# A DLRM tower on one core: gathers tied to TensorE's steps, padded id lines, another order of steps

## The reference

```python
e = jnp.stack([tbl_0[ids[:, 0]], ..., tbl_25[ids[:, 25]]], axis=1)
all_emb = jnp.concatenate([bottom_output[:, None, :], embeddings], axis=1)
gram = jnp.einsum('bfd,bgd->bfg', all_emb, all_emb)
z = gram[:, _TRIU_I, _TRIU_J]
...
h = jnp.concatenate([z, r_bottom_output], axis=1)
h = jnp.maximum(h @ W_top1 + b_top1, 0.0)      # 479 -> 512
h = jnp.maximum(h @ W_top2 + b_top2, 0.0)      # 512 -> 256
y = h @ W_top3                                 # 256 -> 1
```

## Time and profile before

| | us |
|---|---|
| median of 3 runs | 500.98 |
| the runs | 501.84, 500.98, 497.73 |
| the profiled execution: from its first to its last instruction | 370.7 |
| median minus that span | 130.3 |
| PE, PEld, DVE, ACT, POOL busy | 343.2, 282.3, 236.3, 230.8, 257.2 |
| granted clock of TensorE, mean | 0.963 |

### The profile page before, as it was taken

One profiled execution on the slowest core, in us unless ns is written; L12 is line 12 of the kernel. 1 busy time (PEld: TensorE's weight loads), 2 busy tenths in 40 slices (PEclk: granted clock), 3 DMA queues, 4 the chain that ended last, 5 costly groups with the idle time before them and its releaser, 6 DMA issues.

```text
span 370.7 us, 8525 instructions
## 1 busy us (share of the span) xinstructions
PE 343.2 (93%) x3422; PEld 282.3 (76%) x3422; DVE 236.3 (64%) x312; ACT 230.8 (62%) x298; POOL 257.2 (69%) x261
## 2 busy tenths in 40 slices
PE   6899999999699999999999999997977996899996
PEld 5688888887587778788788877776866785677886
DVE  2999999999497769798789945313340332522452
ACT  2699989888497896499997833447321473223222
POOL 5777878777777777777877877777777777770010
PEclk9699999999699999999999999999896999899999
DMA  6977687665957789988767629534593425323200
GB/s 174 249 217 211 194 248 222 190 198 163 319 112 251 205 242 341 287 235 252 230 156 245 191 77 347 176 96 114 152 366 99 115 74 146 97 52 85 66 20 2
DMA packets 48391, 66.86 MB, mean 180 GB/s; under 512 B 15861, under 2 KB 34847, under 8 KB 47840
## 3 DMA queue, kind: packets, MB, share of 16 engines
q1 hardware_dynamic: 40024, 49.32, 43.9%
q0 software_dynamic: 8064, 16.31, 16.7%
q10 hardware_dynamic: 264, 0.69, 0.6%
HBM read 52.36 MB, written 13.93 MB: 179 GB/s over the span
## 4 chain that ended last, share of the span: by engine, by line
PE 69%; POOL 10%; DMA 6%; ACT 5%; issue 5%; DVE 3%; SPq 1%; ACTq 0%; DVEq 0%
PE acc L624 21%; PE acc L625 21%; POOL rows L591 10%; PE gram L655 9%; PE turned L637 6%; PE acc L660 4%; PE acc L661 4%; PE acc L662 4%; DMA rows<-in_tbl,index 2%; DMA wanted<-in_onehot_ids 2%; DVE onehot L899 2%; ACT features L741 1%; ACT staged L823 1%; ACT h L769 1%; DMA square<-products 1%
## 5 line engine op out<-in xcount | busy, mean ns | idle before, releaser
L591 POOL DMA_INDIRECT rows<-in_tbl,index x248 | 253.9, 1024 | 77.7 <-issue 74.4
L899 DVE TENSOR_SCALAR onehot<-wanted,row_number 125x1029 fp32r<-125x1029 int32 (+3 forms) x137 | 151.0, 1150 | 19.6 <-PE acc L625 13.3
L624 PE MATMUL acc<-onehot,table_hi 125*128 125x512 f32 x336 | 136.6, 407 | 3.1 <-DVE table_lo L893 3.1
L625 PE MATMUL acc<-onehot,table_lo 125*128 125x512 f32 x288 | 115.7, 402 | 0.0
L624 PEld LDWEIGHTS acc<-onehot,table_hi 125*128 125x128 f32 x336 | 64.7, 193 | 17.8 <-DVE table_lo L893 3.3
L655 PEld LDWEIGHTS gram<-features 128*54 128x54 f32 x2048 | 60.6, 136 | 17.6 <-issue 14.6
L655 PE MATMUL gram<-features 128*54 128x52 f32 x2048 | 67.5, 222 | 6.0 <-DVE features L925 3.0
L625 PEld LDWEIGHTS acc<-onehot,table_lo 125*128 125x128 f32 x288 | 55.7, 194 | 12.4
L769 ACT ACTIVATE h<-wanted,row_number 125x1029 f32<-125x1029 int32 x42 | 48.8, 1163 | 23.4 <-PE acc L625 20.3
L637 PE MATMUL turned<-identity,rows 128*128 128x128 f32 x248 | 41.8, 294 | 9.9 <-DMA rows<-in_tbl,index 8.1
L772 ACT ACTIVATE onehot<-h,row_number 125x1029 fp32r<-125x1029 f32 x42 | 48.6, 1157 | 1.4
(11 more groups left out here) (49 smaller groups left out, 285.4 us busy)
## 6 DMA issues: line engine op xcount, KB each, us to landing
wanted<-in_onehot_ids SPq DMA_DIRECT2D x20, 514.5 KB, 6.0
parked<-staged SPq DMA_DIRECT2D x32, 256.0 KB, 4.3
table_raw<-in_tbl SPq DMA_DIRECT2D x17, 448.0 KB
looked<-parked SPq DMA_DIRECT2D x2, 2816.0 KB, 12.4
square<-products SPq DMA_DIRECT2D x62, 84.5 KB
rows<-in_tbl,index POOLq DMA_INDIRECT x248
looked<-parked SPq DMA_DIRECT2D x1, 2560.0 KB, 11.0
pairs<-in_tbl SPq DMA_DIRECT2D x3, 448.0 KB
```

The lines of the kernel that those rows point to most:

```text
L591: pool.indirect_dma_start(out=rows[:, n % ROWS_RING, i, :], out_offset=None, in_=gathered[f], in_offset=bass.IndirectOffsetOnAxis(ap=index ...
L624: pe.matmul(to, table_hi[0:ROW_PARTS, v % HIGH_RING, c, :], of, start=(c == 0), stop=False)
L625: last = pe.matmul(to, raw_table(v, low=True)[0:ROW_PARTS, c, :], of, start=False, stop=(c == CHUNKS - 1))
L899: return dve.tensor_scalar(column[:, rows], ids_of(v, slice(0, ROW_PARTS))[:, rows], row_number[0:ROW_PARTS, c:c + 1], None, ALU.is_equal)
```

## The change

1. `order` also lists, for each gather, the step of TensorE that by plan ends at least 3 us (6 us from tile 13 on) before the gather would begin, and GpSimd waits for that step ahead of the gather (`keep_pace`). A wait that repeats the one before it is left out; 192 are left. By the planned lengths gathers 0 to 7 have none, gather 13 waits for column 7 of lookup 0, gather 40 (the first of turn (2, 2)) for column 7 of lookup 4, gather 229 for gram (13, 0), gathers 242 to 244 for gram (14, 0) and 245 to 247 for gram (14, 1).
2. The ids lie in memory in padded lines, as they lie in the core: a partition's copy is one run of 4144 bytes instead of seven of 588 (for lookup 0 one of 2368 and one of 1776).
3. VectorE's round: low half 0 of the next table comes ahead of its columns 0 and 1.
4. The slot-0 fills of the first block come ahead of lookup 9 on VectorE, those of later tiles one tile after another. ScalarE copies the first nine slots of tile 0 (`place_ahead`) ahead of a column of the next lookup instead of after it.
5. The end: turns (15, 2) and (15, 3) come ahead of layer2 of part 2, which is done in two halves, the second after gram (15, 3); an output comes behind the first quarter of the next part's layer1; the pairs of part 3 are loaded after layer1 of part 2; `h2` lies in the place of `table_hi`, so that pairs may be split before the output is done.

```diff
@@ products_and_others
-    steps = [("lookup", v, 0) for v in range(FIRST_LATER)]
+    steps = [("lookup", v, 0) for v in range(FIRST_LATER - 1)]
+    steps += [("bottom", q, 0) for q in range(BLOCK_TILES)] + [("lookup", FIRST_LATER - 1, 0)]
...
-            before += [[] for _ in range(LAYERS_AT[b] - LOOKUPS_AMONG[b])] + layers(b - 1) + [[("output", b - 1, 0)]]
+            before += [[] for _ in range(LAYERS_AT[b] - LOOKUPS_AMONG[b])] + layers(b - 1)
+            before += [[("output", b - 1, 0)]] if b - 1 != APART else []
...
+            if BLOCK_TILES <= chunk[1] + 1 < TILES and chunk[2] == 0:
+                steps.append(("bottom", chunk[1] + 1, 0))
...
+    steps += [("layer2", APART, 1)]
     for part in range(BLOCKS - 1, len(PARTS)):
-        steps += [step for place in layers(part) for step in place] + [("output", part, 0)]
-    return steps
+        steps += begun(part) + [("output", part - 1, 0)] + rest(part)
+    return steps + [("output", len(PARTS) - 1, 0)]
@@ order
+        begins.extend((step[1], gathered - GATHER_LANDS + i * GATHER_LENGTH) for i in range(groups_of(step[1])[step[2]]))
...
+        while step == ("layer2", APART, 0) and turns:
+            turn()
...
+    for t, begin in begins:
+        paces.append(max(((end, step) for end, step in ended if end <= begin - PACE_LEAD[t >= LATE_TILES]),
+                         default=(0, None))[1])
@@ loads of pairs
-PAIRS_AFTER["gram", TILES - 2, TILE_CHUNKS - 1] = (len(PARTS) - 2, 0, BLOCK_TILES - 1)
+PAIRS_AFTER["layer1", APART, M1 - 1] = (len(PARTS) - 2, 0, EARLY_TILES)
+PAIRS_AFTER["gram", TILES - 2, TILE_CHUNKS - 1] = (len(PARTS) - 1, EARLY_TILES, BLOCK_TILES - 1)
@@ ids, SyncE
-                    sp.dma_start(ids_of(v, slice(0, P)), onehot_ids[i:i + 1, first:first + WIDTH].to_broadcast([P, WIDTH])
-                                 ).then_inc(wanted_landed[v % WANTED_RING], 16)
+                    sp.dma_start(to, of.to_broadcast([P, ID_LINE])).then_inc(wanted_landed[v % WANTED_RING], 16)
@@ GpSimd
+            def keep_pace(n):
+                if PACES[n] is None or n and PACES[n] == PACES[n - 1]:
+                    return
+                kind, x, y = PACES[n]
+                if kind == "lookup" and y < CHUNKS - 1:
+                    pool.wait_ge(onehot_used, x * (CHUNKS - 1) + y + 1)
+                elif kind == "lookup":
+                    pool.wait_ge(accumulated, visited(x))
+                else:
+                    pool.wait_ge(grammed, x * TILE_CHUNKS + y + 1)
...
                         f = GROUP * g + i
+                        keep_pace(gathers_before(t) + f)
                         pool.indirect_dma_start(
@@ VectorE
                     if x + 1 < len(VISITS):
+                        table_low_part(x + 1, 0)
                         build(x + 1, (0, 1))
-                        table_low_part(x + 1, 0)
                         build(x + 1, (3,))
...
-                    dve.wait_ge(accumulated, FILL["output", last_on_tiles_of(part), 0] + 1)
+                    dve.wait_ge(accumulated, FILL["layer1", last_on_tiles_of(part), M1 - 1] + 1)
@@ ScalarE
+                    if x == FIRST_LATER - 1:
+                        place_ahead(x)
                     if more:
                         act_chunk(x + 1, ACT_COLUMNS[0])
```

More of the change, by code:

```diff
@@ L49 @@
 WIDE_RING = 6
+ID_LINE = ID_ROWS * ID_PITCH
 FIRST_ROWS = 4
@@ L136, with outputs_of @@
 LAYERS_AT = (None, 10, 10, 8)
+APART = BLOCKS - 2
+def outputs_of(part, i):
+    return (i,) if part == APART else tuple(range(M2))
 LOOKUPS_AMONG = (16, 8, 8, 8)
@@ L153, in layers, with begun, rest @@
         return [[("layer1", part, m)] for m in range(M1)] + [[("layer2", part, 0)]]
+    def begun(part):
+        return [("layer1", part, 0)]
+    def rest(part):
+        return [("layer1", part, m) for m in range(1, M1)] + [("layer2", part, 0)]
     def spread(others, n):
@@ L184, in order @@
     grams = 0
+    begins, ended, paces = [], [], []
     def turn():
@@ L201, in order @@
             turn()
+        while step == ("layer2", APART, 0) and turns:
+            turn()
         steps.append(step)
+        if step[0] == "lookup":
+            ended.extend((now + (c + 1) * LENGTH["lookup"] // CHUNKS, (*step[:2], c)) for c in range(CHUNKS))
         now += LENGTH[step[0]]
         grams += step[0] == "gram"
-    return steps
-ORDER = order()
+        if step[0] == "gram":
+            ended.append((now, step))
+    for t, begin in begins:
+        paces.append(max(((end, step) for end, step in ended if end <= begin - PACE_LEAD[t >= LATE_TILES]),
+                         default=(0, None))[1])
+    return steps, paces
+ORDER, PACES = order()
 def accumulations():
@@ L220, in accumulations @@
         if kind == "layer2":
-            for m in range(M2):
+            for m in outputs_of(b, i):
                 number[kind, b, m] = len(number)
@@ L321, in dlrm_tower @@
         h1_lo = onehot[:, M1 * BLOCK:2 * M1 * BLOCK].rearrange("p (m n) -> p m n", n=BLOCK)
-        h2 = [staged_and[:, :, :, 1 + m, :] for m in range(M2)]
+        h2 = [h2_and[:, m, 0:BLOCK_TILES].rearrange("p q (s t) -> p q s t", s=PACK) for m in range(M2)]
         turned = psum("turned", [P, 2, GROUP, P])
@@ L385, in groups_before, with gathers_before @@
             return sum(len(groups_of(s)) for s in range(t))
+        def gathers_before(t):
+            return sum(sum(groups_of(s)) for s in range(t))
         def rows_count(t, g):
@@ L530, in load_pairs @@
                     sp.wait_ge(accumulated, FILL["layer1", last_on_tiles_of(part), M1 - 1] + 1)
-                for i in range(SP_LOADS if part == len(PARTS) - 1 else len(TRIPLES)):
+                for i in range(SP_LOADS if (part, first, end) == LAST_LOT else len(TRIPLES)):
                     load_triple(sp, b, first, end, i, pairs_landed[part % 2])
@@ L721, in _ @@
                 elif kind == "layer2":
-                    layer2(x)
+                    layer2(x, outputs_of(x, y))
                 elif kind == "output":
@@ L817, in relu1, with relu2 @@
                                      bias=b1_sb[:, m:m + 1]).then_inc(acc_out, 1)
-            def relu2(part):
-                for m in range(M2):
+            def relu2(part, ms):
+                for m in ms:
                     fill = FILL["layer2", part, m]
@@ L959, in split_h1 @@
                 n = width(part)
+                if m == 0 and part:
+                    dve.wait_ge(accumulated, FILL["layer2", part - 1, M2 - 1] + 1)
                 dve.wait_ge(acc_out, FILL["layer1", part, m] + 1)
@@ L1000, in _ @@
                     split_h1(x, y)
[L1001 to L1004, removed]
+                elif kind == "layer2" and y == 0 and x < BLOCKS - 1:
+                    split_bottom(x + 1)
 def layer1_rows():
@@ L1023, in layer1_rows, with id_lines @@
     return at, len(inputs) // 2
+def id_lines(ids):
+    import numpy as np
+    ids = ids.reshape(len(ONEHOT), BLOCKS // VISIT_BLOCKS, VISIT_BLOCKS * BLOCK)
+    rows = np.pad(ids, ((0, 0), (0, 0), (0, WIDTH - VISIT_BLOCKS * BLOCK))).reshape(*ids.shape[:2], ID_ROWS, ID_RUN)
+    lines = np.pad(rows, ((0, 0), (0, 0), (0, 0), (0, ID_PITCH - ID_RUN)))
+    return lines.reshape(*ids.shape[:2], ID_LINE).transpose(1, 0, 2)
 def kernel(**inputs):
```

39 lines of the change are left out of this document (21 added, 18 removed).

## The result

| | median us | runs | profiled span |
|---|---|---|---|
| before | 500.30 | 4 (497.73 to 501.84) | 370.7 |
| after | 432.67 | 4 (431.67 to 433.38) | 431.3 |

After takes 0.8664 of the time of before, 95% interval 0.8614 to 0.8715: faster by 67.6 us, where 7.6 were forecast and the range ended at 488.5.

What follows compares the result with a forecast made beforehand. The prediction took gathers to bound the kernel up to 280.6 us, then TensorE. Span 370.7 - 5.5 (VectorE's round) - 2.1 (end) = 363.1; with 130.3 fixed, 493.4 us, range 488.5 to 501.5.

Steps and rivals of the forecast that it cites:

- With the 130.3 us between its span and the median of 500.98 taken as fixed: Whole kernel: the time outside the profiled span stays constant, so a forecast span of 363.1 us gives 493.4.
- Each gather waits for its step: GpSimd's gathers: the 192 added waits are met before they are reached; taken as 0 us.
- Gaps of GpSimd ended by TensorE: Sign of a wrong forecast: GpSimd idles until TensorE acts, instead of 0.30 us idle before every gather.
- Rival (d): The change doesn't do what it says, as no gather ever waits; contained in all cases at 0, no own chance.
- Low half 0 ahead of columns 0 and 1: VectorE's round, 31.7 to 62.3 us: gathers meet one hit a round instead of three; 5.5 us less.
- The end: TensorE after 280.6 us: idle gaps go under reordered work; sum -2.1 us, between -2.4 and 0.
- Ids 0, fills 0: Start: padded ids gain 1 us, earlier fills some 5 for TensorE; both 0 in the sum, as gathers set the time.
- The gathers set the time up to 280.6: First piece of the kernel: the stream of gathers sets the time; afterwards 90.1 us of TensorE's own work.
- the rivals: Gathers lose as much elsewhere (498.9, chance 0.33), gain more (488.3, 0.08), find a costly step (507.9, 0.09), or never wait.

Runs made afterwards that it cites:

- unstalled session: The one of seven sessions, each run beside the unchanged kernel before, in which that kernel took 374.11 us.
- two looser forms: Kernel before with pacing alone, its waits 20 us looser: 374.44 us; or with one wait a group of up to four gathers: 374.08 us.
- stalled sessions: The six of seven sessions in which the unchanged kernel before took 496 to 509 us.
- pacing alone: Kernel before plus only GpSimd's waits for TensorE's steps ahead of gathers, by the same rule on its own order: 437.54 us.
- fills alone: Kernel before plus a 128x128 fill of GpSimd's own, and a wait for it, ahead of every gather, no pacing: 464.19 us.
- the early and the late waits: Kernel before with pacing's waits on gathers 0 to 39 alone: 491.81 us; on gathers 40 to 247 alone: 461.99 us.

## Why the prediction was wrong, point by point

- **"With the 130.3 us between its span and the median of 500.98 taken as fixed"** is the step that failed. Those us were not outside the span (2 us are); they were TensorE's, in executions that the profile wasn't taken from. Of the 124.2 us between the two spans of before 78.4 are idle time of TensorE (105.9 against 27.5) and 45.8 longer busy time (389.0 against 343.2), in part at half clock (119 us against 27). I saw a gap of a quarter of the time and carried it along as a constant. All terms were then sized in an execution unlike those that the change was timed in.
- **"Each gather waits for its step": "192 waits by nothing are nothing", taken as 0.** The sum in its own frame held: in the unstalled session two looser forms cost 0.3 and 0.0 us (the form of the change itself wasn't met there). In the stalled sessions it is the change: 58.6 us of 67.6. "Gaps of GpSimd ended by TensorE", put down as what would prove me wrong, is what the rows at 37.40 and 44.86 show. Rival (d), that no gather ever waits, is refuted with it.
- **"Low half 0 ahead of columns 0 and 1", -5.5.** The mechanism is there. Between 31.7 and 62.3 us 2 of 21 gathers of after last over 1.3 us, where 12 of 19 did in the trace and 12 of 20 do with pacing alone; I had expected about one in six. But it had a value only while the gathers set the time. In after TensorE waits for no rows; the term is worth nothing there.
- **"The end", -2.1.** The idle times ahead of gram (15, 0) and output 3 (0.91 and 0.57) are gone, as forecast, and 0.57 ahead of output 4 stay. After without pacing, which has this, the fills and the ids, is no faster than before (498.08 against 496.15).
- **Ids 0, fills 0** by the cover of the gathers: without that cover they were to be worth 1 and 5 us. 437.54 to 432.67 leaves room for that, and nothing shows it; gram (0, 0) is at 106.28, not near 93, and 2.04 us of "issue" stand before it.
- **"The gathers set the time up to 280.6"** holds where its profile holds (the row at 285.33) and not in the timed runs, where their stream ends at 428.6 us of 494.9 because it waits for TensorE.
- None of the rivals had gathers that hold up TensorE or its signals. They were weighed for what they do to each other, to VectorE's splits and to the end, never for what they do to an engine that shares no tile with them.

## What to carry to other kernels

Set the span of a profile beside the time of its own run, and of the timed runs, before anything else: if they differ by more than a few us, the profile is of another execution, and no constant bridges it. A stream of gathers that could run ahead freely should be tied to the engine that uses it, gather by gather: here that cost nothing in looser forms where it wasn't needed and gave 13% where it was. Count the records of a trace before you trust a wait that "nothing ends": here the traces with the stops lack about half of them, and the longest stops did end with another engine's work. A saving at one place is kept only if the place behind it is mended too, as the early and the late waits show.

## What the runs showed of the hardware that was not expected

The same program takes 374 or 500 us, for whole sessions at a time; the chip numbered 1 gave 374 in session 3 and 507 in the last, so it isn't tied to a number, and what sets it stays open. In the slower kind TensorE stops, from 0.3 to 23 us (23.31 in after without pacing), and the granted clock falls to half speed behind the long stops (0.63 mean in 29 to 61). The engines that wait for TensorE start late: 1.7 us behind a Gram chunk in place of 0.05, and 10 to 13 us behind a lookup at the long stop. The stops need gathers on GpSimd: with plain transfers of the same bytes they are gone (360.37). Up to gram (0, 0) gaps between gathers are enough to take the long stops away (134.9 to 95.7 with fills alone). Behind it gaps alone save less (334.6 in place of 356.4) than a wait for TensorE ahead of each gather (308.9). Through which shared part a gather reaches TensorE, no run here shows.
